# A routed-expert mixture: TensorE's unrolled expert code becomes one loop, and the routing list is handed out in parts

## What is computed

```python
x = x + xattn(layernorm(x), ctx, ctx, mask, Wq, bq, Wk, bk, Wv, bv, Wqf, Wkf, Wo, bo)
x = x + ffn(layernorm(x), gate_w, w1, w2, w3)

# ffn, E = 8, TOP_K = 2, D = 256, M = 896
probs = softmax(x_flat @ gate_w)
topk_w, topk_idx = top_k(probs, 2); topk_w /= sum(topk_w)
# rows sorted by expert, then for the rows of each expert e:
h = silu(rows @ w1[e]) * (rows @ w3[e])
out_rows = h @ w2[e]
# and each token gets the weighted sum of its two output rows
```

## Time and profile before

| | us |
|---|---|
| three runs | 519.91, 521.49, 524.08 |
| median | 521.49 |
| profiled execution, its own time | 518.49 |
| its span, first to last instruction | 516.7 |
| TensorE matmul busy | 432.2 (84% of the span) |
| VectorE, ScalarE, GpSimd busy | 244.8, 254.5, 217.0 |
| mean granted TensorE clock | 0.918 of full speed |

### The profile page before, as it was taken

How to read it: one execution, slowest core, us unless ns; L and a number is a source line. 1 busy time by engine, 2 the same in 40 slices (tenths; PEclk the granted TensorE clock), 3 DMA queues, 4 the chain that set the end, 5 groups by cost and what they waited for, 6 DMA issues and landing times.

```text
span 516.7 us, 12140 instructions
## 1 busy us (share of the span) xinstructions
PE 432.2 (84%) x4365; PEld 414.0 (80%) x4366; DVE 244.8 (47%) x732; ACT 254.5 (49%) x609; POOL 217.0 (42%) x211
## 2 busy tenths in 40 slices
PE   4999999999989458848999499699889799889940
PEld 3888988988889458838998499699789799889940
DVE  4457877688776725222434034234624324354410
ACT  3677766787556114644534264354455354344320
POOL 4326457664434402673612382382257175122111
PEclk9999999999999858887999699799999979889975
DMA  8461122711281571153451017127222201221111
GB/s 263 141 222 58 43 64 86 274 61 46 67 292 58 128 259 23 32 157 102 120 168 21 23 21 245 35 33 236 42 38 37 43 13 33 42 45 20 33 37 20
DMA packets 35700, 47.54 MB, mean 92 GB/s; under 512 B 3616, under 2 KB 30496, under 8 KB 35616
## 3 DMA queue, kind: packets, MB, share of 16 engines
q1 hardware_dynamic: 22304, 31.82, 18.7%
q0 software_dynamic: 7008, 9.21, 10.7%
q10 hardware_dynamic: 6304, 5.42, 3.8%
HBM read 33.29 MB, written 13.15 MB: 90 GB/s over the span
## 4 chain that ended last, share of the span: by engine, by line
PE 63%; DVE 15%; issue 10%; ACT 6%; ACTq 2%; DMA 2%; POOL 1%; SPq 0%; POOLq 0%; DVEq 0%
PE twin L846 13%; PE bank L832 9%; PE bank L833 9%; PE bank L837 9%; PE twin L677 3%; PE bank L557 3%; DVE bank L1406 2%; PE bank L558 2%; PE bank L559 2%; DVE w_lo L1299 2%; PE twin L689 2%; PE bank L603 2%; PE bank L828 1%; PE bank L581 1%; DVE bank L1401 1%
## 5 line engine op out<-in xcount | busy, mean ns | idle before, releaser
L832 PE MATMUL bank<-c_halves,w_hi 128*128 128x256 f32 x448 | 125.8, 300 | 29.2 <-issue 29.2
L498 POOL DMA_INDIRECT out_rows<-qf,meta x38 | 59.2, 1557 | 160.0 <-ACT qf L1110 111.2
L833 PE MATMUL bank<-c_halves,w_lo 128*128 128x256 f32 x448 | 123.2, 295 | 0.0
L846 PE MATMUL twin<-w_hi,kv_halves 128*128 128x256 f32 x496 | 109.3, 289 | 11.1 <-DVE kv_halves L1410 4.3
L832 PEld LDWEIGHTS bank<-c_halves,w_hi 128*128 128x128 f32 x448 | 90.9, 203 | 30.7 <-issue 30.6
L1406 DVE TENSOR_TENSOR bank<-bank,x_all 128x256 f32<-128x256 f32 (+1 forms) x133 | 54.2, 407 | 128.0 <-ACT x_all L1136 127.8
L846 PEld LDWEIGHTS twin<-w_hi,kv_halves 128*128 128x128 f32 x496 | 86.5, 195 | 13.5 <-DVE kv_halves L1410 9.3
L488 POOL TENSOR_TENSOR w_lo<-raw,w_hi x18 | 77.1, 4282 | 45.3 <-ACT w_hi L1127 45.3
L837 PE MATMUL bank<-c_halves,w_hi 128*128 128x256 f32 x448 | 94.6, 294 | 0.0
L1136 ACT ACTIVATE x_all<-bank 128x256 f32<-128x256 f32 x133 | 51.5, 387 | 81.5 <-PE bank L837 46.8
L833 PEld LDWEIGHTS bank<-c_halves,w_lo 128*128 128x128 f32 x448 | 91.3, 204 | 0.0
(11 more groups left out here) (237 smaller groups left out, 767.1 us busy)
## 6 DMA issues: line engine op xcount, KB each, us to landing
raw<-in_w SPq DMA_DIRECT2D x24, 896.0 KB
x_all<-bucket ACTq DMA_DIRECT2D x36, 129.0 KB, 2.2
raw<-in_ctxT SPq DMA_DIRECT2D x8, 256.0 KB, 2.8
out_rows<-x_all SPq DMA_DIRECT2D x8, 256.0 KB, 2.1
bucket<-pad_rows SPq DMA_DIRECT2D x13, 129.0 KB, 2.7
x_all<-in_x SPq DMA_DIRECT2D x2, 512.0 KB, 6.6
x_all<-bucket SPq DMA_DIRECT2D x6, 129.0 KB, 2.5
x_all<-in_x SPq DMA_DIRECT2D x1, 768.0 KB, 6.8
```

Of the source, the lines that this page charges most:

```text
L498: pool.indirect_dma_start(out=out, out_offset=bass.IndirectOffsetOnAxis(ap=meta[:, v, o, 0:1].bitcast(U32), axis=0), in_=y[:, u, o, :], in ...
L832: nc.tensor.matmul(out_ap, block(w_hi, k), x_hi[:, k, :], start=(k == 0), stop=False)
L833: nc.tensor.matmul(out_ap, block(w_lo, k), x_hi[:, k, :], start=False, stop=False)
L846: last = nc.tensor.matmul(bank[6][:, o * D:(o + 1) * D], stationary[:, c % RING, o * P:(o + 1) * P], w[:, bass.ds(at + (2 * W13 + c * D), D)],
```

## The change

1. **TensorE's mixture** is one `Fori` over four pairs of experts. In its body stand two arms (even and odd expert), each with one copy of a pair unit in a `Fori` over the expert's pairs and one copy of a single. The counts come from a new table `tab_units` (units per expert, in tiles); `tab_pairs`, `tab_odd` and `tab_single_at` are gone. The place of the previous unit's weights, a constant for pairs before, is now read for every unit from `expert_of`, behind its second gate block.
2. **Unit 2's second tile** is loaded from the fixed place behind the first, as soon as the scatters are complete; for that, expert 0 gets 256 padding rows (a second `pad`), the region of each expert becomes 128 rows longer, and SyncE stores only three paddings ahead of these loads and six behind.
3. **The list in parts.** Blocks of unit 1 are spread more evenly, `split_x(2)` comes earlier in it, and VectorE raises `summed` and does unit 2 as soon as 8 tables are there; the rest of the list (`tab_active` to `tab_first`) is worked out behind unit 2. `UNITS_LISTED, ROWS_LISTED, ALL_LISTED` become 4, 8, 12.
4. **Order at the end of the router.** `normalise2` of the last pair stands one block earlier on VectorE; the last `rank` stands one gate block earlier on TensorE, and VectorE takes the last ranks and slots ahead of `block_of(1, 1)`.
5. ScalarE reads the five values of the end (`units_used`, `last_places`) at the end of unit 14, not of unit 2; the wait for all tables stays at unit 2.

```diff
-CAP = T + P
+CAP = T + TWO
-UNITS_LISTED, ROWS_LISTED, ALL_LISTED = 6, 10, 14
+UNITS_LISTED, ROWS_LISTED, ALL_LISTED = 4, 8, 12
...
             sp.wait_ge(list_ready, 1)
-            for e in range(5):
-                pad(e)
+            pad(0)
+            pad(0, P)
+            pad(1)
             for odd in range(2):
                 sp.wait_ge(scattered[odd], 32 * NPR)
-            sp.wait_ge(pad_stored[0], 16)
+            sp.wait_ge(pad_stored[0], 16 * 2)
             sp.wait_ge(meta_ready, 2)
-            sp.dma_start(x_in[:, 0, :], bucket[TWO:TWO + P, :]).then_inc(x_in_loaded, 16)
-            sp.wait_ge(pad_stored[1], 16 * 2)
-            sp.wait_ge(list_ready, ROWS_LISTED)
-            at = sp.value_load(tab_row2[0:1, AHEAD:AHEAD + 1], min_val=0, max_val=PAD_AT)
-            sp.dma_start(x_in[:, 1, :], bucket[bass.ds(at, P), :]).then_inc(x_in_loaded, 16)
-            for e in range(5, E):
+            for o in range(2):
+                sp.dma_start(x_in[:, o, :], bucket[TWO + o * P:TWO + (o + 1) * P, :]).then_inc(x_in_loaded, 16)
+            for e in range(2, E):
                 pad(e)
...
-            def unit(t, e, at_before, single=False):
+            def unit(t, e, slot, single=False):
...
-                down(t - 1, MB - 1, at_before)
+                before_it = pe.value_load(expert_of[0:1, bass.ds(t - 1, 1)], min_val=0, max_val=E - 1)
+                down(t - 1, MB - 1, pe.snap((before_it % 2) * WALL))
...
-            gate_up(1, e1, 2)
             rank(NPR - 1)
+            gate_up(1, e1, at1, 2)
...
             pe.wait_ge(list_ready, UNITS_LISTED)
-            for e in range(E):
-
-                of = e * NT + (3 if e < 2 else 1)
-                start = pe.value_load(tab_start[0:1, e:e + 1], min_val=AHEAD, max_val=MOST)
-
-                def pairs_if_listed(j):
-                    with pe.If(pe.value_load(tab_pairs[0:1, of + 2 * j:of + 2 * j + 1], min_val=0, max_val=1)):
-                        unit(start + j, e, (e if j else max(e - 1, 0)) % 2 * WALL)
...
-                pairs_if_listed(0)
-                with pe.If(pe.value_load(tab_odd[0:1, e:e + 1], min_val=0, max_val=1)):
...
+            with pe.Fori(0, E // 2) as r:
+                for s in range(2):
+                    e = 2 * r + s
+                    start = pe.value_load(tab_start[0:1, bass.ds(e, 1)], min_val=AHEAD, max_val=MOST)
+                    units = pe.value_load(tab_units[0:1, bass.ds(e, 1)], min_val=1, max_val=NT + 1)
+                    pairs = pe.snap(units // 2)
+                    with pe.If(pairs):
+                        with pe.Fori(0, pairs) as j:
+                            unit(start + j, e, s * WALL)
+                    with pe.If(units % 2):
+                        unit(start + pairs, e, s * WALL, single=True)
...
                 if t == AHEAD:
                     act.wait_ge(list_ready, ALL_LISTED)
+                if t == SURE - 2:
                     count.extend((units_used(act), last_places(act)))
...
             block_of(0, 4)
+            normalise2(NPR - 1)
             block_of(0, 5)
             rank_slots(NPR - 2)
-            normalise2(NPR - 1)
...
             block_of(1, 0)
-            block_of(1, 1)
             dve.wait_ge(list_step, 1)
             rank_slots(NPR - 1)
             slots(NPR - 1)
+            block_of(1, 1)
...
-            nc.vector.tensor_copy(tab_pairs[:], more.rearrange("a e n -> a (e n)")).then_inc(list_ready, 1)
...
+            nc.vector.tensor_copy(tab_units[:], n_tiles[:]).then_inc(list_ready, 1)
...
             nc.vector.tensor_copy(tab_row2, lists[:, 8, :]).then_inc(list_ready, 1)
-            block_of(1, 5)
+            dve.wait_ge(list_ready, ROWS_LISTED)
+            dve.sem_inc(summed, AHEAD * MB)
+            mix(AHEAD)
             link(nc.vector.tensor_scalar(active, unit_no[:], ends[:, 3, E - 1:E], None, ALU.is_lt))
...
             dve.wait_ge(list_ready, ALL_LISTED)
-            dve.sem_inc(summed, AHEAD * MB)
-            units_of_mixture(dve, mix)
+            units_of_mixture(dve, mix, AHEAD + 1)
```

More of the change, by code:

```diff
@@ L6 @@
 P = 128
+TWO = 2 * P
 T, D = 2048, 256
@@ L157, in build @@
             kf[0:1, 1, (10 + i) * UNITS:(11 + i) * UNITS].bitcast(I32) for i in range(7))
+        expert_of = kf[0:1, 1, 12 * UNITS:12 * UNITS + MOST + E + 4].bitcast(I32)
         x_hi, x_lo = c_hi, c_lo
@@ L208, in settle, with units_of_mixture @@
             eng.sem_inc(gate_pass, 1)
-        def units_of_mixture(eng, step):
-            for t in range(AHEAD, SURE):
+        def units_of_mixture(eng, step, first=AHEAD):
+            for t in range(first, SURE):
                 step(t)
@@ L802, in x_transposes, with gate_up @@
                 last.then_inc(xT_done, 1)
-            def gate_up(t, e, c, single=False):
+            def gate_up(t, e, slot, c, single=False):
                 if c == 0:
@@ L1554, in _ @@
                                          steps[:], ALU.is_gt))
-            nc.vector.tensor_copy(tab_pairs[:], more.rearrange("a e n -> a (e n)")).then_inc(list_ready, 1)
             nc.vector.tensor_reduce(n_tiles[:, 2:E], more[:, 2:E, :], AX.X, ALU.add)
             link(nc.vector.tensor_reduce(n_tiles[:, 0:2], more[:, 0:2, 2:NT], AX.X, ALU.add))
+            block_of(1, 2)
             pairs_of = more.rearrange("a e (j h) -> a e j h", h=2)[:, :, :, 1]
@@ L1569, in _ @@
                 link(nc.vector.tensor_tensor(ends[:, i + 1, by:E], ends[:, i, by:E], ends[:, i, 0:E - by], ALU.add))
-            link(nc.vector.tensor_scalar(n_row[:], ends[:, 3, :], float(AHEAD - 1), None, ALU.add))
-            nc.vector.tensor_copy(tab_single_at[:], n_row[:]).then_inc(list_ready, 1)
-            link(nc.vector.scalar_tensor_tensor(out=n_tiles[:], in0=n_row[:], scalar=1.0, in1=ends[:, 0, :],
+            link(nc.vector.scalar_tensor_tensor(out=n_tiles[:], in0=ends[:, 3, :], scalar=float(AHEAD), in1=ends[:, 0, :],
                                                 op0=ALU.add, op1=ALU.subtract))
             nc.vector.tensor_copy(tab_start[:], n_tiles[:]).then_inc(list_ready, 1)
-            block_of(1, 3)
+            block_of(1, 4)
             link(nc.vector.tensor_tensor(past, unit_no[:].rearrange("a (t o) -> a t o", o=1).to_broadcast([1, UNITS, E]), wide(ends[:, 3, :]), ALU.is_ge))
@@ L1579, in _ @@
             nc.vector.tensor_copy(tab_expert, lists[:, 1, :]).then_inc(list_ready, 1)
+            block_of(1, 5)
             link(nc.vector.tensor_tensor(past_odd, past, wide(n_odd[:]), ALU.mult))
@@ L1585, in _ @@
             nc.vector.tensor_copy(tab_single, lists[:, 8, :]).then_inc(list_ready, 1)
+            block_of(1, 6)
+            split_x(2)
             link(nc.vector.tensor_scalar(lists[:, 9, :], lists[:, 8, :], -1.0, 1.0, ALU.mult, ALU.add))
             nc.vector.tensor_copy(tab_double, lists[:, 9, :]).then_inc(list_ready, 1)
-            block_of(1, 4)
             link(nc.vector.scalar_tensor_tensor(out=n_tiles[:], in0=ends[:, 0, :], scalar=-float(TWO), in1=cap_step[:],
@@ L1606, in _ @@
             link(nc.vector.tensor_scalar(used[:, 1:2], used[:, 0:1], -float(SURE), None, ALU.add))
-            block_of(1, 6)
-            split_x(2)
             link(nc.vector.tensor_tensor(is_last, active[:, 0:MOST], active[:, 1:MOST + 1], ALU.subtract))
```

80 lines of the change are left out of this document (33 added, 47 removed).

## The result

| | before | changed kernel |
|---|---|---|
| median of runs, us | 521.02 (519.91 to 524.08, 4 runs) | 497.65 (493.89 to 502.33, 4 runs) |
| ratio | | 0.952, interval 0.944 to 0.959 |
| changed kernel timed again, other chips | 520.27, 519.54 | 492.03 (ratio 0.949), 491.58 (ratio 0.948) |

The kernel became 4.8 to 5.2% faster. The measured 497.65 lies inside the forecast's range (475 to 513).

What follows compares the result with a forecast made beforehand. TensorE was taken as bound, with 41.3 us of pauses from jumps over unneeded code. Terms summed to -36.0: 518.5 profiled to 482.5, plus 3.0 for the median of runs, 485.5 us; range 475 to 513.

Steps and rivals of the forecast that it cites:

- The loop and back jumps at next to nothing: TensorE's loop: seven inner back jumps cost 0, each outer one 0.3 us with its border; no block dropped after use.
- A: Rival: program blocks are fetched again on back jumps of TensorE's loop; 510 us in runs, chance 0.15.
- C: Rival: each back jump, inner ones too, costs 5.1 us like jumps under the weights' transfer; 541 us, chance 0.10.
- Rival B: Converters become the bound: TensorE waits at experts' first units for ScalarE's casts and GpSimd's parts; 508 us, chance 0.10.
- The price of jumps under the weights' transfer: Ahead of expert 2: two jumps cost 10.17 us while weights cross, against 3.5 to 4.0 at other borders.
- Unit 2 (-7.6 from `tab_count` on): Unit 2 starts at 181.0 instead of 189.23, -8.2 us in all, 0.6 of it ahead of `tab_count`.
- the list starts 0.6 earlier: End of the router: reordering `normalise2`, the last rank and `block_of(1, 1)` starts the list 0.6 us earlier.
- Units 2 and 3 (-9.4): Unit 4, expert 2's first, starts 36.3 us behind unit 2's start instead of 45.7.
- Rival D: The list in parts brings nothing, since late tables delay what holds unit 2 or 3; 494 us, chance 0.13.
- The other borders: Pauses become 0.3: -7.5 us ahead of expert 3, -3.7 of 4, -3.2 of 6; half-rate slow starts, four times -0.5.
- The five reads (+1.0): ScalarE's reads behind unit 14 add 2.6 us on ScalarE, of which 1.0 passes to TensorE.
- The end (-1.0): TensorE's pause at the last single falls from 2.9 to 1.9 us.

Runs made afterwards that it cites:

- e2: Changed kernel with TensorE's outer loop written out as eight expert blocks: 492.71 us, ratio 0.951 to the kernel before.
- e1: The changed kernel timed again without an edit: 492.03 us, ratio 0.949 to the kernel before.
- f3: Changed kernel with TensorE's outer loop as two rounds of four experts instead of four rounds of two: 498.31 us, ratio 0.957 to the kernel before.
- f4: e2 with two never-entered copies of the pair's code between each expert's pairs and its single: 528.51 us, ratio 1.014 to the kernel before.
- e7: Changed kernel with VectorE finishing the whole list ahead of unit 2: 488.50 us, ratio 0.943 to the kernel before.
- e4: Kernel before with only TensorE's loop, `tab_units` and `expert_of` added, all else as before: 491.4 us, ratio 0.951 to the kernel before.
- e3: Changed kernel with ScalarE's five table reads back at the end of unit 2: 490.41 us, ratio 0.947 to the kernel before.
- e8: Changed kernel with ScalarE's first weight casts for an expert behind `evacuate_y`, the second one block later: 491.85 us, ratio 0.952 to the kernel before.
- e5: Changed kernel with ScalarE's five reads moved into the middle of unit 15, behind its fourth block: 487.20 us, ratio 0.939 to the kernel before.
- f1: Changed kernel with the edits of e5 and e7 together: 488.70 us, ratio 0.943 to the kernel before.
- f2: The changed kernel a third time, without an edit, on the chip of f1: 491.58 us, ratio 0.948 to the kernel before.
- e6: Changed kernel with four of the six late paddings stored ahead of SyncE's wait for the scatters: 492.78 us, ratio 0.952 to the kernel before.

## Why the prediction came out as it did

**The loop and back jumps at next to nothing: right.** From expert 2 on no block is fetched in a round (about four were forecast for the stretch), and no pause stands between two pairs, so the inner back jumps cost nothing that can be seen. The outer back jump, put at 0.3 with its border, shows as 0.4 us: 0.85 and 0.80 ahead of experts 4 and 6 against 0.43 and 0.38 in e2. Rivals A and C are out. Rival B is there in small: the waits of L846 for ScalarE, its sign, went from 3.8 to 10.5 us. The prediction weighed its free back jumps against the two-page window of the Trainium skill, "Runtime: NRT & Kernel Launch", section "Instruction fetch mechanics". By that rule every outer back jump (over 3.7 blocks) would fetch its page first; the trace disagrees, with no block behind 220.1 in e1. The 128 KiB that the Trainium skill gives TensorE in the same section would be, as an estimate from that page, eight blocks of 16 KiB; f3's loop of about 7.3 blocks, which can lie across eight or nine with what stands on either side, did not stay, which neither confirms nor contradicts that figure.

**The reason for the gain: right in the main.** The prediction said that jumps over unneeded code cost, and f4 shows it. It gave the gain to two things together, nothing long to jump over and a loop that goes back only to blocks already used; e2 shows that the second brings nothing once an expert's code is short.

**The price of jumps under the weights' transfer: not settled.** The prediction took the 10.17 us for the effect of DMA engines that are 70% busy with weights. In f4 a border costs 6.9 to 7.6 at a DMA share of 0.46 as at 0.15, so up to there the pause goes with the number of blocks that must come one after another. But the 10.17 us pause had a higher share, 0.82 with all transfers:

```profile
224.80:234.90 10.10, 0.00 (x0) 0.00 (x0) 0.42 (x1) 1.87 (x4) 5.89 (x2) 0.64 0.82 278
```

Its two blocks came at 225.1 and 230.8, 5.7 us apart where f4 has 4.1 at most, and the first matmul came 4.1 us behind the second and not 1.1. No run repeats that share at a long jump, so the prediction's reason stays possible for this one pause. For the total it did not matter, since the pause went with the jump.

**Unit 2 (-7.6 from `tab_count` on): right, -8.6.** The step "the list starts 0.6 earlier" failed. Timeline of TensorE in e1, answering to the first of the earlier trace rows:

```profile
156.24 0.63 PE L660 MATMUL bank<-ident,rows 128*128 128x128 f32 x4 [1.64 <-DVE slot_of L1363]
```

It waited 1.54 for `normalise2` and now waits 1.64 for `rank_slots`, ahead of which `normalise2` was put: the wait changed its name. The start of `tab_count` scatters between 165.3 and 168.3 over the profiles of all versions, but for the two at 171.70 and 172.65, so the +1.7 in the table can't be put down to the change.

**Units 2 and 3 (-9.4): -6.2, mis-sized by a wait that was called even.** "ScalarE waits for it where it read five values before: even" overlooked that ScalarE's load, its casts and y of unit 3 stand behind that wait. e7 takes the late table away and gives 3.1 us. Rival D named this mechanism (unit 3 held by late tables). By e4 and e3, which have the five reads at the same place, 4.4 of the 4.9 us that unit 2 had won were given back by unit 4; by e7 the late table cost 4.9 behind unit 2 for 1.8 won at it; that the median of 492 to 498 is near D's 494 has other shortfalls in it as well.

**The other borders: the pauses right, the slow starts wrong.** Ahead of experts 3, 4 and 6 the pauses of 7.82, 4.03 and 3.53 became 0.43, 0.85 and 0.80: 13.3 us gone where 14.4 were forecast. Of the four slow starts (2.4 each), 0.5 each was to stay as a gain. Expert 3 to 4 gave -2.9 instead of -4.2 and expert 4 to 5 -0.3 instead of -1.5. Part of that is pauses: 0.85 instead of 0.3 ahead of expert 4, and 1.64 ahead of expert 5 where 1.29 was to stay. The rest is the lateness of ScalarE, put at 1.9 from one row: the two units of expert 3 took 0.3 us more than before and not 0.5 less, clock and all. e8, the one other order tried, does not remove it.

**The five reads (+1.0): mis-sized.** Expert 6 to 7 came out at +2.6 against -0.5. e5, with the reads where ScalarE has slack, makes that stretch 3.9 us shorter: the 2.83 us wait and the clock behind it, at its lower level for 3.4 us in e1, are gone. With units 2 and 3 this is the largest miss, 3 us each.

**The end (-1.0): -1.9, by another way and in part by luck.** TensorE's last pause fell from 2.88 to 0.55, but the end hangs on ScalarE, whose instruction stream is late there; by its code it then jumps out of its own nested branches, which no run tests. Timeline of ScalarE, before and e1:

```profile
500.76 0.84 ACT L1110 ACTIVATE qf<-twin,meta 128x256 f32<-128x256 f32 x2 [5.67 <-issue]
...
474.15 0.84 ACT L1100 ACTIVATE qf<-twin,meta 128x256 f32<-128x256 f32 x2 [5.27 <-issue]
```

From there to the end of the span are 15.9 us, before as after. That row should have been looked for before costing TensorE's pause there. Of the 1.9 us, 0.4 are in this idle time. The other 1.5 are the clock behind the start of expert 7, which fell to its lower level in the profiled execution of the kernel before, 29 matmuls in the first 5 us where e1 has 42:

```profile
462.10:467.10 5.00, 4.96 (x29) 4.99 (x30) 0.94 (x3) 1.07 (x3) 0.00 (x0) 0.66 0.23 58
```

It fell in f1 too and not in e1 or f2, so these 1.5 us can go either way from one execution to the next.

**SyncE's paddings at 0: right** within what can be seen. TensorE waited 0.8 us for unit 3's rows in e1; e6, with the paddings ahead, is no faster and no slower.

## What to carry to other kernels

A jump over code that isn't run has a price by the blocks that must come behind it, here about 3.5 us a block and, with two unused copies of a unit to jump over, seven us a border (f4). Having one copy of the long code, in a loop over the expert's pairs, so that only short code is jumped over, removes it, and whether the outer loop is rolled matters little. A loop whose body is too long for the program memory pays at its back jump (5.8 us in f3). When a pause of the bound engine (the one that sets the time, here TensorE) goes away, look at once what stood in its shadow: here a helper engine's table reads, its wait for a late table and its casts took back about a fifth of the expected gain. Moving five reads by a few operations gave more (3.9 us) than the list and rows in parts (0.5).

## What the runs showed of the hardware

- Program blocks that are needed in turn behind a jump come 3.1 to 4.1 us apart (f4; 3.1 and 3.7 in the kernel before at experts 4 and 6), and once 5.7 (before, at expert 2, with a DMA share of 0.82). Behind a short jump, a block that comes 1.2 us ahead of its first matmul adds nothing to the pause: 0.40 with it (e2), 0.43 without (e1).
- A loop of about 3.7 blocks ran the 15 units from unit 4 on with no block fetched (e1), and its outer back jump cost 0.4 us (0.85 and 0.80, against 0.43 and 0.38 in e2); one of about 7.3 blocks was fetched again in its second round (f3).
- Table reads by ScalarE cost about 0.6 us each where nothing hides them (an estimate: 5.38 less 2.50 for five, e1 and e5).
- At the start of expert 7 the granted clock stayed at its upper level behind a pause of 1.55 us (e1) and fell behind one of 1.62 (f1) and one of 1.04 (before), so a pause of that length is worth between nothing and 1.5 us more than itself.
